# A one-core graph transformer layer: ternary weight sets spread over later items, and the subtractions after clipping moved to GpSimd

## The reference, cut to what matters

```python
xn = _layernorm(x, axis=-1)
x = x + _L0_gnn_ref(xn, src, dst, ...) + _L0_mix_ref(xn[None], ...)[0]
x = x + _L0_ffn_ref(_layernorm(x, axis=-1)[None], L0_ffn_w1, L0_ffn_w2)[0]

def _quant_weight(w):                      # w1 is 4096 x 1024, w2 is 1024 x 4096
    s = jnp.clip(jnp.mean(jnp.abs(w)), EPS, None)
    wq = jnp.clip(jnp.round(w / s), -1.0, 1.0) * s
    return w + jax.lax.stop_gradient(wq - w)

h = jax.nn.gelu(_bitlinear(x, w1), approximate=False)   # activations rounded to 8 bits too
return _bitlinear(h, w2)
```

## Time and profile before

| what | value |
|---|---|
| median of 3 runs | 1316.63 us (1312.86 to 1319.8) |
| the profiled execution | 1312.0 us, its span 1310.2 us |
| granted TensorE clock, mean | 0.999 |
| PE busy | 1292.4 us, 99% of the span |
| DVE, ACT, POOL busy | 843.6, 654.0, 94.6 us (64%, 50%, 7%) |

### The profile page before, as it was taken

How to read it: one execution, slowest core, us unless ns; L and a number is a source line. 1 busy time by engine, 2 the same in 40 slices (tenths; PEclk the granted TensorE clock), 3 DMA queues, 4 the chain that set the end, 5 groups by cost and what they waited for, 6 DMA issues and landing times.

```text
span 1310.2 us, 18779 instructions
## 1 busy us (share of the span) xinstructions
PE 1292.4 (99%) x6370; PEld 614.3 (47%) x6370; DVE 843.6 (64%) x1471; ACT 654.0 (50%) x897; POOL 94.6 (7%) x91
## 2 busy tenths in 40 slices
PE   9999999999999999999999999899999999999999
PEld 5454444555445544444444444344444444444444
DVE  6854542352576868966983654344876878886774
ACT  7765565364313246523442753646862277465460
POOL 0000000000000002200000101232440000000000
PEclk9999999999999999999999999999999999999999
DMA  8498887864134556715876999998759829723523
GB/s 353 145 280 268 272 273 221 304 209 176 48 134 171 190 197 193 225 66 196 282 251 219 200 250 217 295 297 303 246 176 345 249 59 284 190 54 90 129 56 105
DMA packets 203093, 269.10 MB, mean 205 GB/s; under 512 B 110464, under 2 KB 144000, under 8 KB 199424
## 3 DMA queue, kind: packets, MB, share of 16 engines
q1 hardware_dynamic: 190432, 255.93, 61.9%
q10 hardware_dynamic: 11136, 6.82, 2.3%
q0 software_dynamic: 1440, 5.24, 2.2%
HBM read 184.33 MB, written 57.67 MB: 185 GB/s over the span
## 4 chain that ended last, share of the span: by engine, by line
PE 80%; DMA 7%; DVE 5%; SPq 4%; ACT 2%; issue 1%; DVEq 0%; ACTq 0%
PE ps L2243 36%; PE ps L2565 9%; PE ps L2374 8%; PE ps L2667 8%; PE ps L2630 7%; PE ps L2524 7%; PE ps L2443 2%; DMA S<-SPLIT 2%; DMA S<-HL 1%; PE ps L2382 1%; PE ps L2295 1%; DMA STREAM<-in_w1t 1%; SPq L581 1%; DMA HL<-in_w1t 1%; DMA w1q_scratch<-STREAM 1%
## 5 line engine op out<-in xcount | busy, mean ns | idle before, releaser
L2243 PE MATMUL ps<-S,XH 128*128 128x512 f16 x1440 | 317.1, 379 | 0.4 <-DVE Zb L1659 0.4
L2243 PEld LDWEIGHTS ps<-S,XH 128*128 128x128 f16 x1440 | 139.9, 98 | 165.3 <-DVE Zb L1659 2.7
L2243 PE MATMUL ps<-S,Zb 128*128 128x512 f16 x480 | 106.4, 379 | 0.0
L2374 PE MATMUL ps<-XH,S 128*128 128x512 f16 (+1 forms) x576 | 102.6, 339 | 0.0
L2243 PE MATMUL ps<-Zb,XH 128*128 128x512 f16 x432 | 94.8, 379 | 0.0
L1002 ACT ACTIVATE AT<-ps 128x320 f16<-128x320 f32 x40 | 17.4, 435 | 143.1 <-PE ps L2243 143.1
L1612 DVE TENSOR_SCALAR STREAM<-tables,keys 128x320 f16 x240 | 71.0, 296 | 24.6 <-PE ps L2443 13.2
L2524 PE MATMUL ps<-XH,AT 128*128 128x512 f16 x400 | 86.7, 379 | 0.0
L2524 PE MATMUL ps<-Zb,AT 128*128 128x512 f16 x400 | 86.5, 379 | 0.0
L2374 PEld LDWEIGHTS ps<-XH,S 128*128 128x128 f16 x576 | 56.1, 98 | 47.0 <-issue 2.3
L802 ACT ACTIVATE STREAM<-STREAM 128x1024 f32<-128x1024 f32 x64 | 66.8, 1045 | 12.1 <-DMA STREAM<-in_w1t 10.0
(11 more groups left out here) (317 smaller groups left out, 1992.2 us busy)
## 6 DMA issues: line engine op xcount, KB each, us to landing
STREAM<-in_w_all SPq DMA_DIRECT2D x48, 512.0 KB, 5.2
STREAM<-in_w1t SPq DMA_DIRECT2D x42, 512.0 KB, 5.2
STREAM<-in_w2t SPq DMA_DIRECT2D x30, 512.0 KB, 5.1
XIN<-in_x SPq DMA_DIRECT2D x20, 512.0 KB, 5.2
w2q_scratch<-STREAM SPq DMA_DIRECT2D x15, 512.0 KB, 4.2
Zb<-in_w1t SPq DMA_DIRECT2D x14, 512.0 KB, 7.2
blocks_scratch<-S SPq DMA_DIRECT2D x4, 1792.0 KB, 8.4
blocks_scratch<-STREAM SPq DMA_DIRECT2D x4, 1792.0 KB, 8.4
```

The costliest lines, as they stand in the source:

```text
L2243: last = mm(acc[:, n * BANK:(n + 1) * BANK], left(l, kc), right(kc, r)[:, n * BANK:(n + 1) * BANK], start=(kc == 0 and i == 0), stop=(kc = ...
L2374: last = mm(ps[:, 3 * j * BANK + a:3 * j * BANK + b], Wq_s[:, kc, l, mc], XH[:, r, kc, a:b], start=(kc == 0 and l == 0 and r == 0), stop=( ...
```

## The change

Four edits. (1) The table of the items: items 1, 2, 3 and 5 get 1, 2, 2, 3 sets in place of 2, 3, 2, 2, so that 20 sets in place of 21 lie in the items, and set 30 joins set 31 in the x1 stage; `cuts` has its own numbers for items 2 and 3. The third set of item 5 is now a `CLIPPED` one. (2) The operation that makes blocks 4 and 6 goes from VectorE to GpSimd, ahead of the two that are there; waits count one operation of VectorE and three of GpSimd per set. (3) One load moves ahead of the loads of the second weight's blocks. (4) `y_round(8)` moves behind the first two copies of its `f1_act`.

```diff
-LAST_QUADS = 31
+LAST_QUADS = 30
...
-        ST_COUNTS = (0, 2, 3, 2, 0, 2, 3, 3, 3, 3)
+        ST_COUNTS = (0, 1, 2, 2, 0, 3, 3, 3, 3, 3)
...
-        X1_QUADS = {1: 31}
+        X1_QUADS = {1: 30, 3: 31}
...
-                    sp.wait_ge(S("made"), 2 * k + 1)
+                    sp.wait_ge(S("made"), k + 1)
...
-                sp.wait_ge(S("made_last"), 2 * i + 2)
+                sp.wait_ge(S("made_last"), 3 * i + 3)
...
+            quad_load(last_s1 + 3)
             z1_block(0)
             quad_store(last_s1)
             for n in range(1, 6):
                 z1_block(n)
-            quad_load(last_s1 + 3)
...
-                pool.wait_ge(S("made"), 2 * i + 2)
+                pool.wait_ge(S("made"), i + 1)
+                nc.gpsimd.tensor_tensor(made[:, 4:8:2, :], made[:, 1:4:2, :], made[:, 0:2, :], ALU.subtract,
+                                        saturate=False).then_inc(S("made_last"), 1)
+                pool.wait_ge(S("made_last"), 3 * i + 1)
...
-                cuts = (2, 2, 2, 2, 4, 8) if i == 1 else (2, 4, 5, 6, 8, 12)
+                cuts = {1: (2, 2, 2, 2, 4, 4), 2: (0, 0, 0, 0, 2, 8), 3: (2, 4, 4, 4, 6, 8)}.get(i, (2, 4, 5, 6, 8, 10))
...
-                for part in {0: (0, 1), 1: (2, 3)}.get(t, ()):
-                    quad_round(LAST_QUADS, part)
+                if t < 4:
+                    for part in range(2 * (t % 2), 2 * (t % 2) + 2):
+                        quad_round(LAST_QUADS + t // 2, part)
...
             y_std(8)
-            y_round(8)
-            f1_act(1, 0, [lambda: y_round(9)], [lambda: y_std(9)])
+            f1_act(1, 0, [lambda: y_round(9)], [lambda: y_round(8), lambda: y_std(9)])
...
-                dve.wait_ge(S("made"), 2 * i + 1)
-                V.tensor_tensor(made[:, 4:8:2, :], made[:, 1:4:2, :], made[:, 0:2, :], ALU.subtract,
-                                saturate=False).then_inc(S("made"), 1)
```

More of the change, by code:

```diff
@@ L768, in last_blocks @@
                 made = blocks_made(i)
-                pool.wait_ge(S("made"), 2 * i + 2)
+                pool.wait_ge(S("made"), i + 1)
+                nc.gpsimd.tensor_tensor(made[:, 4:8:2, :], made[:, 1:4:2, :], made[:, 0:2, :], ALU.subtract,
+                                        saturate=False).then_inc(S("made_last"), 1)
+                pool.wait_ge(S("made_last"), 3 * i + 1)
                 nc.gpsimd.tensor_tensor(made[:, 5, :], made[:, 3, :], made[:, 4, :], ALU.subtract,
                                         saturate=False).then_inc(S("made_last"), 1)
-                pool.wait_ge(S("made_last"), 2 * i + 1)
+                pool.wait_ge(S("made_last"), 3 * i + 2)
                 nc.gpsimd.tensor_tensor(made[:, 7, :], made[:, 2, :], made[:, 5, :], ALU.subtract,
```

## The result

The changed kernel takes 1308.81 us in the median of 13 runs (1306.84 to 1311.68); the kernel before, measured between them, 1314.62 (1312.19 to 1323.51). The ratio is 0.995, with an interval of 0.9934 to 0.9967. Measured again later, beside the last experiments, it gave 1309.28 against 1316.32, ratio 0.9954 (0.9938 to 0.997). So 5.8 and 7.0 us go by the medians, where 7.2 was forecast. The profiled execution took 1311.2 us, span 1309.4, 2.4 above its kernel's median; another execution is shown with experiment 8.

What follows compares the result with a forecast made beforehand. TensorE, busy 99% of the span, was taken as the bound, waiting mostly for ScalarE's copies. 1312.0 - 9.3 + 0.1 + 0.6 + 1.4 = 1304.8 us, 1309 as a median; forecast 1307.6 to 1310.6 (chance 0.50), whole range 1302 to 1317.

Steps and rivals of the forecast that it cites:

- Items 1 to 3, 9.3 us: New tables remove TensorE's waits at P6(2), P5(2), P5(3) and a slow product: 9.3 us gained.
- P4(2), 0.1: In item 2, set 11's clipping ahead of c22(2) on VectorE costs 0.1 us, bounds 0 and 1.
- The operation on GpSimd, 2.2: The moved operation of 1024 columns takes 2.2 us on GpSimd, between 1.1 and 2.2.
- the paragraph on the changed profile: Expected profile after the change; among others, GpSimd's operation takes 2.2 us alone, 3 and more beside VectorE.
- Items 6 to 9, 0.6, and the shared access: VectorE and GpSimd blocking each other in items with three sets costs 0.15 us per item, 0.6 in all, bounds 0 and 7.6.
- the rival's 0.25: Chance 0.25 that VectorE and GpSimd's shared access becomes the bound in items 6 to 9: 2 to 7.6 us lost, 1312.6.
- the other half of the paragraph: Items 6 to 9: first set's store leaves 1.0 us later, third set starts up to 1.5 later; c21 shifts -0.9 to +0.6.
- a sign that it is wrong: Third sets' clipping (L1711) waiting for stores was listed among the observations that would show the prediction wrong.
- Early sets, 0: Sets ahead of the items, in the counting stage: the moved operation costs nothing there.
- `edge_sum(0)`, 1.4: At the end of the items, item 9's last low half comes late for `edge_sum(0)`: 1.4 us lost, bounds 0 and 3.
- `y_round(8)`, 0: Feed-forward part: P6's 1.3 us wait goes but reappears ahead of a later product; gain 0, bounds 0 and 1.3.
- Slower, by the stores' landing: Third sets wait for first sets' stores; landing after 7.7 us, not 4.3, loses 16 us, 1323. Chance 0.07.

Runs made afterwards that it cites:

- experiment 8: The changed kernel measured and traced again, 1309.28 us, ratio 0.9954; also with its early load put back, 1311.25 us, ratio 0.9965.
- experiment 1: The changed kernel with VectorE making blocks 4 and 6 again in every set (tables, load and `y_round(8)` as changed): 1306.23 us, ratio 0.9944.
- experiment 4: The changed kernel with GpSimd making blocks 4 and 6 only in sets 0 to 14, 30 and 31, VectorE in the others: 1308.23 us, ratio 0.9944.
- experiment 5: The changed kernel with a third buffer for a set's eight blocks from set 15 on: 1306.13 us, ratio 0.9941.
- experiment 10: The changed kernel with GpSimd's operation in set 11 alone, a third buffer, and item 6's cuts (0, 2, 2, 2, 4, 10): 1308.17 us, ratio 0.9933.
- experiment 2: The kernel before with only the operation moved to GpSimd; tables, early load and `y_round(8)` as before: 1315.32 us, ratio 1.0008.

## Why the prediction was right, point by point

*Items 1 to 3, 9.3 us.* Right: the three waits and the slow product are gone, and experiment 1 shows that the tables alone do it. From start to start they were 9.8, half a us more than the sum of the brackets. The step of 2.61 in the prediction is 2.59: the last of the eight products that it was read from starts 0.16 late beside its bracket of 0.78. Nothing hangs on the difference.

*P4(2), 0.1.* Right by the working: one clipping ahead of c22 fits in two steps, with no wait in either trace of the changed kernel. It is an edge: 0.45 in experiment 4 with the same order in item 2, and 0.93 in experiment 1 with one operation of 1.23 more.

*The operation on GpSimd, 2.2.* 2.00 to 2.01 alone and 2.37 to 2.39 beside VectorE in the changed kernel (2.92 once in experiment 5); 3 and more, as the paragraph on the changed profile had it, was too much. The nearest bound was the right one: the cost goes with the columns. The estimate from the Trainium skill (GPSIMD Engine Reference, 3.1 Elementwise) was 2.25, and the trace has 2.00.

*Items 6 to 9, 0.6, and the shared access.* The sum was mis-sized: 1.0 and 2.3 in two traces, 1.6 and 2.9 from start to start, inside the bounds. The mechanism that I gave first was the wrong one of two. I weighed how long the engines block each other, and put the rival's 0.25 on it. By the Trainium skill (SBUF — State Buffer, Who interferes with whom) one engine holds the shared ports for a whole instruction; the rows bear out the blocking, and experiment 5's stretch from 912.99 to 919.07, 6.1 us for 2.44 + 4.19 us of work, the nine tenths. But experiment 5 blocks more and has none of these waits. What cost time was the other half of the paragraph: the first set's store leaves later, and the third set waits for it. I had the store leaving 1.0 later after the clipping and the third set starting up to 1.5 later, inside the slack; in item 6 they are 1.7 and 4.1, because the blocking, which I had priced as time of the two engines over a whole item, lengthens the clipping and the store's chain too. Against that I had VectorE 0.9 shorter behind that start, and it is 2.8 shorter, since the late set finds GpSimd idle. Two wrong sizes met: c21 comes 1.25 later where -0.9 to +0.6 was forecast. L1711 waiting for stores stood in the prediction as a sign that it is wrong. The sign came (5.24 in item 6, 2.92 to 5.62 in items 7 to 9), and its price stayed small for this reason. And the largest part in the first trace, P5(6), belonged to no term: a third set in item 5 moves set 18's load and passes, which I had priced at nothing.

*Early sets, 0.* Not quite nothing on VectorE. In the stage of the count matrix its 240 small operations of 128 columns (L1617, L1614 before) take 80.1 us where they took 69.2. In the seven traces with the operation on GpSimd there they take 79.8 to 80.6, in the six others 69.2 to 70.1. A row shows how:

```profile
519.34 2.00 POOL L770 TENSOR_TENSOR Zb<-Zb 128x1024 fp8e4<-128x1024 fp8e4 x1 [8.81 <-DVE Zb L1714]
519.38 2.01 DVE L1617 TENSOR_SCALAR STREAM<-tables,keys 128x128 f16 x1
...
525.52 0.24 DVE L1617 TENSOR_SCALAR STREAM<-tables,keys 128x128 f16 x1
```

An operation of 0.24 us takes 2.01 beside GpSimd's. TensorE has a new wait of 0.2 to 0.3 there in three of the seven traces (0.18 at 524.36 in the first), so the 0 was off by little.

*`edge_sum(0)`, 1.4.* Right: 1.58 and 1.60 in that sum, and gone with the third buffer, so the cause named (the buffer's store) is shown.

*`y_round(8)`, 0.* Right in the sum, half right in the rows: not 0 and 1.6 but 0.62 and 0.82, since a later copy takes over half of the wait.

*Slower, by the stores' landing.* It did not come: the store in item 6 landed after 4.3 us as before. But experiment 5 shows that this rival had hold of the right chain, with a smaller price, and what lengthens the chain is GpSimd's part ahead of the store and not its landing.

*The sum.* 7.2 was forecast, 5.8 and 7.0 measured. By the stage's rows, from start to start, it is 9.8 - 2.9 - 1.75 = 5.1 in the first trace and 9.8 - 1.6 - 1.75 = 6.4 in the second, before the late loads are counted. That the time itself came out so close, 1309 against 1308.81, is in part luck: the kernel before measures 1314.62 over 13 runs and not the 1316.6 of three that the forecast started from, 2.0 less, and the gain is 1.4 less, so the two nearly cancel.

## What to carry to other kernels

A store that frees a buffer starts when the last engine of the chain is done. When an operation goes to a slower engine, follow the buffer's turn-round (the operation, the store's issue, its landing) before the busy times: here VectorE lost 18 us of work and waited longer for a buffer, and a third buffer took away the waits of TensorE that came of it. Where two engines block each other, look for it in that chain too, and not only in the sum of their work. On an engine that runs in written order, a pass whose load may be late belongs behind the work that others wait for; moved one place it saved the wait, moved further it made a wait of 2.71 in the next item. And where single transfers land late in some executions and not in others, take a second trace before a wait of 1 to 2 us is given a cause.

## What the runs showed of the hardware

- GpSimd's subtraction of fp8 blocks took 1.09 us for 512 columns and 2.00 for 1024; an estimate from these two leaves 0.18 for a fixed part. On VectorE the one of 1024 took 1.23.
- VectorE's and GpSimd's operations beside each other took turns: VectorE's 1.22 became 2.00 or 2.79, GpSimd's 1.09 became 1.95, and a VectorE operation of 0.24 took 2.01 beside one of 2.00. VectorE's sums that read PSUM (c21, c11) kept their 0.74.
- The granted clock, and what TensorE did before: idle 2.22 ahead of P5(3) in the kernel before, and 2.25 in experiment 4, and the product behind took 2.76 and 2.75 (clock 1.00: 2.4 GHz). Idle 2.71 in experiment 10: 4.45. Idle 4.42: 4.45. Idle 5.88 in experiment 2: 5.30. The last stretches, after 5.88 and after 2.71:

```profile
832.40:837.70 5.30, 5.25 (x13) 1.96 (x14) 2.73 (x4) 3.90 (x4) 4.31 (x4) 0.50 1.05 372
```

```profile
926.33:930.78 4.45, 4.45 (x13) 1.68 (x14) 1.10 (x2) 2.02 (x2) 2.57 (x2) 0.62 1.03 339
```

A clock of 0.50 is 1.2 GHz for all of the product, 0.62 for most of it.
